# Attention values product: both halves copied by ScalarE at the top of a head, summed on GpSimd

## What is computed

```python
def attention(q, k, v, Wc, bc):
    qh = q.reshape(b, s, N_GROUPS, HEADS_PER_GROUP, HEAD_DIM).transpose(0, 2, 3, 1, 4)
    scores = jnp.einsum('bghsd,bgtd->bghst', qh, kh) * scale
    probs = jax.nn.softmax(scores, axis=-1)
    out = jnp.einsum('bghst,bgtd->bghsd', probs, vh)
    return out.transpose(0, 3, 1, 2, 4).reshape(b, s, D_MODEL) @ Wc.T + bc

x = x + attention(layernorm(x), ctx_512, ctx_512, Wc, bc)
x = x + experts(layernorm(x), gate_kernel, gate_proj, up_proj, down_proj)
```

## Time and profile before

| | us |
|---|---|
| median of 3 runs | 9768.41 |
| lowest, highest | 9763.69, 9772.23 |
| the profiled execution | 9766.52 |
| its span, first to last instruction | 9764.4 |

### The profile page before, as it was taken

How to read it: one execution, slowest core, us unless ns; L and a number is a source line. 1 busy time by engine, 2 the same in 40 slices (tenths; PEclk the granted TensorE clock), 3 DMA queues, 4 the chain that set the end, 5 groups by cost and what they waited for, 6 DMA issues and landing times.

```text
span 9764.4 us, 171795 instructions
## 1 busy us (share of the span) xinstructions
PE 9171.4 (94%) x44592; PEld 7700.9 (79%) x44593; DVE 6407.9 (66%) x10304; ACT 4437.6 (45%) x7458; POOL 5273.7 (54%) x5081
## 2 busy tenths in 40 slices
PE   7888888888895999999999999999999999999999
PEld 5777666667674788888888888888888888888888
DVE  6777777777775566666655666656666566656565
ACT  6666666666663333333333333333333333333333
POOL 3444444444444565666655665656665555655564
PEclk9999999999997999999999999999999999999999
DMA  2111111111112455555544555546555455555454
GB/s 88 48 50 49 53 50 48 48 50 54 47 47 63 107 112 119 126 117 113 116 106 106 129 114 111 112 107 135 113 116 110 105 110 114 132 109 112 111 124 81
DMA packets 664525, 918.17 MB, mean 94 GB/s; under 512 B 338193, under 2 KB 477457, under 8 KB 663954
## 3 DMA queue, kind: packets, MB, share of 16 engines
q0 software_dynamic: 209920, 604.72, 28.8%
q1 hardware_dynamic: 454162, 308.44, 12.1%
HBM read 1064.79 MB, written 376.45 MB: 148 GB/s over the span
## 4 chain that ended last, share of the span: by engine, by line
PE 60%; DMA 4%; issue 1%; DVE 1%; ACT 1%; SPq 1%; POOL 0%; DVEq 0%; ACTq 0%; POOLq 0%
PE bank L1520 39%; PE bank L1543 21%; DMA gu_raw<-in_L_ffn_up_proj 4%; SPq L1255 1%; ACT gu_hi L1354 1%; DVE gu_lo L1434 0%; ACT xT_hi L1347 0%; DVE h_lo L1451 0%; DVE h L1446 0%; POOL xg L1307 0%; DVE xT_lo L1428 0%; DVE h_hi L1449 0%; DVE xT L1423 0%; PE bank L1570 0%; DVEq L41 0%
## 5 line engine op out<-in xcount | busy, mean ns | idle before, releaser
L1307 POOL DMA_INDIRECT xg<-xn_rows,gather_row x2304 | 2753.5, 1195 | 2081.4 <-PE bank L1520 1452.4
L1520 PE MATMUL bank<-xT_hi,gu_hi 128*128 128x512 f32 (+2 forms) x6912 | 2553.7, 369 | 100.9 <-DVE xT_lo L1428 87.2
L1520 PE MATMUL bank<-xT_lo,gu_hi 128*128 128x512 f32 (+2 forms) x6912 | 2543.9, 368 | 0.0
L1520 PE MATMUL bank<-xT_hi,gu_lo 128*128 128x512 f32 (+2 forms) x6912 | 2543.7, 368 | 0.0
L1365 ACT ACTIVATE gated<-bank 128x512 f32<-128x512 f32 x432 | 258.4, 598 | 3042.0 <-PE bank L1520 3042.0
L1520 PEld LDWEIGHTS bank<-xT_hi,gu_hi 128*128 128x128 f32 x6912 | 1299.6, 188 | 278.0 <-issue 89.9
L1319 POOL DMA_INDIRECT out_rows<-rows_out,entry_now x576 | 1139.6, 1978 | 681.5 <-DVE rows_out L1458 322.6
L1520 PEld LDWEIGHTS bank<-xT_lo,gu_hi 128*128 128x128 f32 x6912 | 1299.8, 188 | 159.0
L1520 PEld LDWEIGHTS bank<-xT_hi,gu_lo 128*128 128x128 f32 x6912 | 1299.4, 188 | 158.6
L1446 DVE TENSOR_TENSOR h<-bank,gated 128x512 f32<-128x512 f32 x432 | 297.7, 689 | 1588.9 <-ACT gated L1365 1588.9
L1543 PE MATMUL bank<-d_hi,h_hi 128*128 128x512 f32 x3162 | 1256.0, 397 | 73.4 <-DVE h_lo L1451 73.3
(11 more groups left out here) (162 smaller groups left out, 14635.2 us busy)
## 6 DMA issues: line engine op xcount, KB each, us to landing
gu_raw<-in_L_ffn_gate_proj SPq DMA_DIRECT2D x576, 384.0 KB
gu_raw<-in_L_ffn_up_proj SPq DMA_DIRECT2D x576, 384.0 KB
d_raw<-in_L_ffn_down_proj SPq DMA_DIRECT2D x144, 1536.0 KB
xg<-xn_rows,gather_row POOLq DMA_INDIRECT x2304
x_t<-in_x SPq DMA_DIRECT2D x64, 512.0 KB, 4.8
inv_wide<-inverse_sums SPq DMA_DIRECT2D x512, 64.0 KB
out_rows<-x SPq DMA_DIRECT2D x64, 512.0 KB, 5.4
xn_rows<-xn SPq DMA_DIRECT2D x64, 512.0 KB, 6.4
```

Of the source, the lines that this page charges most:

```text
L1307: pool.indirect_dma_start(out=xg[:, m, :], out_offset=None, in_=quarter_rows, in_offset=bass.IndirectOffsetOnAxis(ap=gather_row[:, m:m + 1 ...
L1520: last = nc.tensor.matmul(bank[:, 0:cols], w[:, c, n, j * P:(j + 1) * P], v[:, c, 0:cols], start=(c == 0 and w is gu_hi and v is xT_hi), s ...
```

## The change

ScalarE copies both halves of the group's values product, 64x512 each, to one tile `o_halves`, at the top of the head, ahead of the head's own copy and exponential. VectorE's `sum_out` is gone. GpSimd makes the two sums of 64x256 from `o_halves` ahead of its multiply in `normalise_out`; before the first of them it waits for both copies and for three kinds of earlier work of its own, before the multiply for its own sums. Where TensorE waited for the sums before it wrote into the bank again, it now waits for the copies.

```diff
-            o_low = sb(attention_mem, "o_low", [HEAD_DIM, 512], F32)
+            o_halves = sb(attention_mem, "o_halves", [HEAD_DIM, 2, 512], F32)
...
-                def normalise_out(i, g):
+                def normalise_out(i, g, earlier):
 
                     n = G * i + g
+                    hold(out_copied, 2 * n + 2)
+                    for before in earlier:
+                        hold(*before)
+                    for r in range(2):
+                        hi, low = (o_halves[:, part, :].rearrange("p (a two t) -> p a two t", two=2, t=P)[:, :, r, :]
+                                   for part in range(2))
+                        pool.tensor_tensor(o_sum[HEAD_DIM * r:HEAD_DIM * (r + 1), :, :], hi, low, ALU.add).then_inc(osum_ready, 1)
                     hold(osum_ready, 2 * n + 2)
...
-                            normalise_out(t.i - OUT_SUM[h][0], OUT_SUM[h][1])
+                            normalise_out(t.i - OUT_SUM[h][0], OUT_SUM[h][1],
+                                          ((xbias_ready, t.i + 1 + (h > 6 and t.next)), (ln1_ready, 2 * (t.i + 1 + (h > 2 and t.next))),
+                                           (ln2_ready, 2 * (t.i - 1 + (h > 10)) if t.back1 else 0)))
...
-                def copy_out_low(i, g):
+                def copy_out(i, g):
 
                     act.wait_ge(pv_done, G * i + g + 1)
                     wait(act, osum_ready, 2 * (G * i + g))
-                    act.activation(o_low[:, :], O_BANK[g % 2][HEAD_DIM:P, :], ACT.Copy).then_inc(olow_copied, 1)
+                    for part in range(2):
+                        act.activation(o_halves[:, part, :], O_BANK[g % 2][HEAD_DIM * part:HEAD_DIM * (part + 1), :], ACT.Copy
+                                       ).then_inc(out_copied, 1)
...
                     for h in range(H):
+                        if h in OUT_SUM and (t.back1 or not OUT_SUM[h][0]):
+                            copy_out(i - OUT_SUM[h][0], OUT_SUM[h][1])
                         copy_probs_hi(i, h)
...
-                        if h in OUT_SUM and (t.back1 or not OUT_SUM[h][0]):
-                            copy_out_low(i - OUT_SUM[h][0], OUT_SUM[h][1])
...
-                def sum_out(i, g):
-
-                    dve.wait_ge(olow_copied, G * i + g + 1)
-                    wait(dve, onorm_ready, G * i + g)
-                    for r in range(2):
-                        hi, low = (o.rearrange("p (a two t) -> p a two t", two=2, t=P)[:, :, r, :]
-                                   for o in (O_BANK[g % 2][0:HEAD_DIM, :], o_low[:, :]))
-                        dve.tensor_tensor(o_sum[HEAD_DIM * r:HEAD_DIM * (r + 1), :, :], hi, low, ALU.add).then_inc(osum_ready, 1)
...
-                    wait(pe, osum_ready, 2 * (G * (SC * b - 1) + g + 1))
+                    wait(pe, out_copied, 2 * (G * (SC * b - 1) + g + 1))
...
-                        wait(pe, osum_ready, 2 * (G * i + g - 1))
+                        wait(pe, out_copied, 2 * (G * i + g - 1))
```

More of the change, by code:

```diff
@@ L193, in moe_block @@
             pt_done, pthi_copied, ptlo_copied = sem("pt_done"), sem("pthi_copied"), sem("ptlo_copied")
-            pv_done, olow_copied, osum_ready = sem("pv_done"), sem("olow_copied"), sem("osum_ready")
+            pv_done, out_copied, osum_ready = sem("pv_done"), sem("out_copied"), sem("osum_ready")
             othi_ready, otlo_ready = sem("othi_ready"), sem("otlo_ready")
@@ L411, in _ @@
                 for g in (G - 2, G - 1):
-                    normalise_out(TILES - 1, g)
+                    normalise_out(TILES - 1, g, ())
                 scatter(TILES - 2, range(TOP_K))
@@ L539, in _ @@
                 for g in (G - 2, G - 1):
-                    copy_out_low(TILES - 1, g)
+                    copy_out(TILES - 1, g)
                     split_out_hi(TILES - 1, g)
@@ L690, in tile @@
                         copy_probs_lo(i, h)
-                        if h in OUT_SUM and (t.back1 or not OUT_SUM[h][0]):
-                            sum_out(i - OUT_SUM[h][0], OUT_SUM[h][1])
                         if h in OUT_SPLIT and (t.back1 or not OUT_SPLIT[h][0]):
@@ L724, in _ @@
                 for g in (G - 2, G - 1):
-                    sum_out(TILES - 1, g)
                     split_out_lo(TILES - 1, g)
```

## The result

The changed kernel takes 9864.62 us (9857.11 to 9868.04, 3 runs) against 9768.41 before: a ratio of 1.0099, with a 95% interval of 1.0085 to 1.0112. It is slower, as forecast, by 96 us where 46 were forecast. The profiled execution has a span of 9855.4 us. From the first tile's normalise to the last's it is 84.5 us longer than before (3007.7 against 2923.2), so the loss lies in the attention stage.

The account below looks back on a forecast made before the run. No attention-stage engine is full; ordered queues of ScalarE and VectorE wait for one another. Span 9764.4 + 41 (tiles, end) + 7 (clock) = 9812; with profiled execution and median each 2 above, 9815 us; range 9750 to 9875.

Parts of the forecast that it names:

- The price of the sum: Each GpSimd sum of 64x256 was taken at 0.74 us, between bounds of 0.37 and 0.9.
- cheap sums: Rival: GpSimd's sums cost under the break-even of 0.56 us; at 0.45 the kernel takes about 9740 us; 20%.
- dear ones: GpSimd sums at the upper bound of 0.9 us add 41 us, 9856; part of a rival given 15%.
- head 0: VectorE's queue up to head 2's statistics comes 1.34 us earlier; copies fit ScalarE's idle time, GpSimd has nothing to do.
- Head 4, group 3: GpSimd's sums behind the factors leave 0.63 us of the 1.34 relief; ScalarE's split starts at 1601.52 against 1602.15.
- Heads 6 to 9, group 0: Sums queue behind queries, bias and a scatter; the split comes 0.11 us later, and VectorE's earlier work buys nothing.
- Head 12: ScalarE has no gap, so the second copy adds 0.62 us; the next middle tile begins 0.73 later, 45.2 against 44.5.
- The other tiles: A batch's last tile loses 0.39 us, its first 0.54; a batch 2.4 us, 16 batches 38 us.
- The clock: TensorE's longer waits bring low-clock stretches on the dense part; 7 us taken, bounds none and 43 us.
- a relief that ends in a wait for GpSimd: In heads 6 to 9, VectorE's whole relief was said to end in ScalarE's split waiting for GpSimd.
- Rival B: Sums are dearer or meet VectorE's two-input instructions; one meeting per tile at 0.32 us adds 20 us, 9835; 15%.
- a sign against it: In the trace after, no two-input instruction of VectorE should be longer than before.

Follow-up runs that it names:

- e13: The changed kernel with scatters 5 to 7 moved from heads 14 and 15 to head 1 of the next tile, behind group 2's sums: 9826.55 us.
- e9: The changed kernel with GpSimd's bias addition moved from head 6 to head 1 of the tile that needs it: 9782.07 us.
- e17: e13 with the next tile's bias addition also moved, to head 14; the split of group 0 stays in head 9: 9724.67 us.
- e2: The kernel before, plus a copy of the upper half in head 12 alone, into a buffer nobody reads: 9808.16 us.
- e1: The kernel before with only ScalarE's low copy moved to the top of the head; VectorE still makes both sums: 9681.01 us.
- e15: e1 with the bias addition moved to head 1, as in e9: 9740.24 us.
- e16: e13 with the bias addition moved to head 5, behind group 3's multiply, and the split of group 0 to head 11: 9871.44 us.
- e3: The changed kernel with the sums given back to VectorE, reading both halves from SBUF; both copies stay at the top: 9732.48 us.
- e11: The changed kernel with five idle matmuls of 512 columns in TensorE's wait ahead of the transposes of xn2: 9897.68 us.
- e12: The kernel before with the same five idle matmuls as e11, as a control: 9813.14 us.
- e6: The changed kernel with GpSimd's last scatters one head earlier, two at head 13, two at head 14, none at head 15: 9911.74 us.
- e18: e1 with scatters 5 to 7 moved to head 1, as in e13: 9671.77 us.

## Why the prediction was right in direction and wrong in size

**The price of the sum: right.** 0.733 us for 0.74. From start to start, two queued sums took 0.81 rather than 0.68, 0.13 per group more. So neither rival that rests on the price, cheap sums or dear ones, came true.

**The step that failed: head 0.** The prediction said of GpSimd "has nothing to do there" and let VectorE's whole relief, 1.34 us, reach the factors. GpSimd had two scatters there, and they waited for ScalarE's pT_hi of head 15. The relief at the factors was 0.43 us in the tile shown. Two things share the difference. One is the order in the queue: in the tile from 901.79 it holds ScalarE's split back by 0.57 us and leaves 1.17 of the relief. The other is that pT_hi of head 15 comes 1.2 us late in ten of 28 middle tiles, the shown one among them, and the scatters with it; the prediction has no term for that, and its cause is open. e13 moves the scatters, and both are gone. Then the prediction's chain holds: the factors end at 20.78 us (-1.40), group 3's split stands at 23.80 (-0.66, forecast -0.63), group 0's at 37.02 (+0.17, forecast +0.11), and the tile takes 45.12 us (forecast 45.2). Over 28 middle tiles the mean grew by 0.78 us in e13 and by 1.71 in the changed kernel, for 0.73 forecast; e13 takes 9827 us, 38 less, for a forecast of 9815. The scatters were in the timeline of before; only the idle time ahead of the copies was looked at, on ScalarE.

**Head 4, group 3.** Forecast 0.63 earlier, measured 0.61 later, 1.24 apart: 0.91 from the smaller relief, 0.33 from the chain, whose two sums end later and whose wait ahead of the multiply was 0.73 here and is 0.44 in most tiles (in e13 the chain took 3.02 us for 2.99 forecast).

**Heads 6 to 9, group 0.** From split to split the forecast was 13.13 us, measured 13.23. The mechanism was right: the bias addition and a scatter stand ahead of the sums. Its weight was not seen. The step says that VectorE's relief "buys nothing"; it did not ask what the chain would be worth if the queue were changed. e9 and e17 put it at 83 and 102 us, about as much as the whole loss.

**Head 12.** Forecast +0.62 from group 0's split to the normalise, measured +0.45 (8.10 for 7.65); e2 has +0.47 for the same copy alone. Of the 1.90 us by which the tile is longer, 1.17 were not forecast: 0.91 + 0.33 + 0.10 - 0.17.

**The other tiles.** Where keys begin, the shortest tiles are 47.52 for 46.97, just the 0.54 forecast; the mean rose by 1.21. Across the loop's end it is 0.87 for 0.39.

**The clock, and a term that is missing.** The forecast put 7 us on the clock. In ten of the 42 tiles at the first three places of a batch the granted clock of the first 10 us was 0.84 to 0.86 (before: in none), and they are 0.9 to 1.2 us longer than the shortest kind (45.5 us for a middle tile, 47.5 where keys begin): 10 us in all, so the size was about right. This is read from the tiles, and no run changes the clock alone. In 22 others the clock was 0.93 or more, and ScalarE took pT_hi of head 15 or of head 0 about 1.2 us late; they are 0.5 to 1.8 us longer, some 18 us in all. The prediction has no term for these. The shortest kind itself is 1.0 us longer than before in a middle tile, for 0.73 forecast.

**The waits that the change removes.** The earlier trace rows has VectorE waiting 147.3 us for ScalarE's low copy. The prediction used 0.35 of it in head 0 and took the 0.87 of head 4 as part of the sum's old place. In e1 both are gone and a middle tile is 1.2 us shorter, their sum, by moving one line. The change contains that gain of 88 us and spends it: 51 on a second copy that e1 does not need, 132 in GpSimd's queue. The prediction saw the two as one, a relief that ends in a wait for GpSimd, and not that the moved copy is a gain by itself.

**Rival B, the meeting with VectorE.** In the change itself it is small: `hot` got shorter (0.603 us in the mean for 0.715), and the values' split went from 0.426 to 0.656 us, 56 times in all, 13 us; the prediction had named a longer two-input instruction of VectorE as a sign against it. But e15 and e16 show its full size. The Trainium skill's rule (SBUF — State Buffer, Who interferes with whom) is that a VectorE instruction with two SBUF inputs contends with a GpSimd instruction that reads SBUF, and that the shared port pair is an exclusive lock; the trace agrees, since oT_lo ended 0.28 us after the bias addition in e15 and 0.29 after it in e16, however early it had begun.

## What to carry to other kernels

Before a step is moved to an engine that looks idle, list what stands ahead of the new place in that engine's queue and what each of these waits for, DMA issues too: the sums themselves cost what was forecast, and the loss came from two scatters and one addition ahead of them. Take a change apart and run its cheapest part alone; here one moved line was worth 88 us by itself, and the rest of the change 183 in loss. When work is moved on GpSimd, look which two-input instruction of VectorE it will then run beside.

## What the runs showed of the hardware

- A VectorE instruction with two SBUF inputs beside a GpSimd addition of 128x1024 took 1.35 and 2.12 us instead of 0.43, and ended just after it.
- A fall of TensorE's clock from 2.4 to 1.2 GHz in the dense part behind the normalise costs a tile 1.2 to 1.5 us in e3 and e17, and about 1.0 in the changed kernel. In e3 such tiles take 45.10 us at a granted clock of 0.96, the others 43.90 at 1.00.
- Idle matmuls in TensorE's wait left the granted clock of the whole stage at 0.93 (e11). Behind the normalise fewer tiles had a low clock (one of 42 for ten), but no time was won there, and the tile across the loop's end grew by 2.9 us in e11 and in e12: 33 and 44 us in all.
- TensorE's signals can be seen late. In e1, e3 and the changed kernel ScalarE often took pT_hi of head 15 at 6.2 us instead of 5.0, in e6 VectorE the logits 2.1 us later, while TensorE's records stood where they had been. With the scatters moved (e13, e18) or the bias moved (e9, e15) they came in time in the tiles that kept the full clock; with the idle matmuls of e11 too. In e1 it cost nothing that can be told: its middle tiles take 43.3 us with it and e18's 43.3 without it. In the changed kernel it delays the scatters ahead of group 2's sums, and such tiles are 0.9 us longer. What causes it stays open.
